# Edge sums of a graph network: packed bank offsets, edge weights moved to ScalarE, and 10 instead of 17 wide products of zeros in a pass

## The chip, the cores and the metric

One core of a Trainium2 chip runs the whole program. The metric is the device time of one launch in microseconds. TensorE multiplies, VectorE, ScalarE and GpSimd work on tiles in SBUF and PSUM, SyncE issues most DMAs. Each engine has a sequencer that reads its instructions in order.

## The reference

200,000 edges (src, dst) over 12,500 nodes with 64 features, three layers:

```python
f1 = relu(x[row] @ nb_W[l] + nb_b[l]); f2 = relu(x[col] @ self_W[l] + self_b[l])
h = relu(concat([f1, f2], 1) @ att1_W[l] + att1_b[l])
log_alpha = (h @ att2_W[l] + att2_b[l])[:, 0]
mask = clip(sigmoid(log_alpha) * (ZETA - GAMMA) + GAMMA, 0, 1)
rowsum = segment_sum(mask, row) + 1e-06
d = clip(rowsum ** -0.5, 0, 10)
vals = mask * d[row] * d[col]
x = segment_sum(vals[:, None] * x[col], row)
out = out + x
```

`row` is src, `col` is dst. The result is a layer norm of x + out.

## The kernel before

First the edges are sorted on the chip by their row, in blocks of 128 nodes, and padded, so that each tile of 128 edges has the rows of one block. This gives 1664 tiles. Eight tiles (U) make a step, four steps a pass of 32 tiles: QUADS is 52 passes per layer. `block_of` holds the block of each tile.

Each layer has three stages. The node stage makes per-node terms. The edge stage gathers them for each edge, makes the mask and, by one-hot products, the row sums. Between 9512 and 10576 us of the third layer, and at the same place of the others, stands the third stage, the edge sums. It is the stage that the change touches, and its loop is the pass of 32 tiles, called a lap here. A lap has three K steps (i = 0, 1, 2), whose edge rows x[col] were kept in DRAM (`kept_x`) and are loaded to `k_x`, and one G step, whose rows are gathered by GpSimd from `y_table` (already multiplied by d of the column). For a K step the engines do this:

- SyncE loads `k_cols` of step k+2, the column numbers of its edges (line 379), as soon as the look-up of step k-1 is done, and then `k_x` of step k (line 393).
- ScalarE (lines 683 and 687, steps i = 0 and 2) or VectorE (line 947, step i = 1) makes from them the transposed column one-hots `look_t` of step k+2.
- TensorE, `pick_rows` (line 564): 24 products of the one-hots with `d3`, which is d in three bf16 parts, in two halves. Each half goes to its own bank.
- VectorE, `look_up` (line 958): picks from each tile's bank the value of its column's high part and sums it, which is d of the column, into `k_weight`.
- VectorE, `weigh`: copies eight row numbers (967), multiplies `k_weight` by the mask (969) and makes for each tile a row one-hot times the weight (973), `k_hot`.
- TensorE, `sum_edges` (called at 601): for each of the eight tiles the product of `k_hot` and `k_x`, 128x64 in f32 (two passes each), added into a bank at a column offset. The offset is 64 times the tile's block less the first block of the step. The eight offsets stand in registers that `spots` fills from `spot_of` by one load of 16 (line 578) at i = 0 and one at i = 2.
- VectorE, `join` (981): adds the bank to `acc` at the step's first block, whose number comes by a register load of one.

The G step is like it, but ScalarE scales the gathered rows by the mask (672), in two halves, and VectorE makes one wide one-hot without weights (782). Its sum is the fourth of the lap (613).

Every bank is cleared by a product of zeros of 512 columns before its sum (`clear`). `stay_busy` adds such products into an unused bank. With four clears, and 2 + 2 in each K step and 1 before the G sum, a lap has 17 of them.

The order is the program order of each engine. In TensorE's lap: for each i: clears, sum of step k, register load at i = 0 and 2, pick of step k+2, at i = 1 the G sum, two products of zeros. VectorE's body for i: at i = 1 the G one-hot and the compare of line 947; look-up of step k+1; weigh of step k+1; join of step k-1; register load; at i = 2 the G join. ScalarE's and SyncE's bodies, and VectorE's, hold two laps (`B_BODIES`).

Of the kernel before, what the change touches and what calls it, by code (L numbers as in the profile page):

```python
# [26 lines left out]
I32 = mybir.dt.int32  # L27
ALU = mybir.AluOpType
# [27 lines left out]
def build(nc, x, src, dst, nb_W, nb_b, self_W, self_b, att1_W, att1_b, att2_W, att2_b, out):  # L56
# [53 lines left out]
    with ctx:  # L110
# [54 lines left out]
        spot_of = sb("spot_of", [1, TILES + 2 * U], mybir.dt.int16)  # L165
# [54 lines left out]
        def in_p3(shape, dt):  # L220
# [56 lines left out]
        k_rows, k_sel, k_wt, k_w, g_xs, k_acc = (  # L277
            sem("k_rows"), sem("k_sel"), sem("k_wt"), sem("k_w"), sem("g_xs"),
# [174 lines left out]
        def _(pe):  # L453
# [34 lines left out]
            spot = [[pe.alloc_register(f"pe_spot{h}_{k}") for k in range(2 * U)] for h in range(2)]  # L488

            with pe.Fori(0, LAYERS) as l:  # L490
# [85 lines left out]
                def spots(h, at):  # L576

                    pe.load(spot[h], spot_of[0:1, ds(at, 2 * U)])

                def sum_edges(to, j, hot, rows):  # L580
                    at = [pe.snap(r, min_val=0, max_val=(U - 1) * HID)
                          for r in spot[j // 2][j % 2 * U:(j % 2 + 1) * U]]
                    for k in range(U):
                        last = plus(to[:, ds(at[k], HID)], hot[:, k, :], rows[:, k, 0:HID])
                    return last
# [5 lines left out]
                spots(0, 0)  # L591
                with pe.Fori(0, QUADS) as b:
                    m = l * QUADS + b
                    for i in range(3):
# [3 lines left out]
                        stay_busy(2)  # L598
                        pe.wait_ge(k_w, l * (K_STEPS + 1) + k + 1)
                        pe.wait_ge(k_xin[i], (l * QUADS + (b + 1)) * 16)  # L600
                        sum_edges(bank[i], i, k_hot[i], k_x[i]).then_inc(k_o[i], 1)
                        if i == 0:
                            spots(1, (b * 4 + 2) * U)
                        if i == 2:
                            spots(0, (b * 4 + 4) * U)
                        pick_rows(b, i + 2)
                        if i == 1:
                            pe.wait_ge(g_acc, m)
                            clear(bank[3])
                            stay_busy(1)  # L610
                            pe.wait_ge(g_w, m + 1)
                            pe.wait_ge(g_xs, (m + 1) * 2)
                            sum_edges(bank[3], 3, g_hot, g_x).then_inc(g_o, 1)
# [5 lines left out]
        def _(act):  # L619
# [6 lines left out]
            with act.Fori(0, LAYERS) as l:  # L626
# [63 lines left out]
                with act.Fori(0, B_BODIES) as b:  # L690
                    for i in range(6):
                        if i % 3 != 1:
                            look_onehot(b, i + 2)

                        if i % 3 != 1:
                            continue
# [16 lines left out]
        def _(dve):  # L713
# [142 lines left out]
            v.memset(spot_of[0:1, TILES:TILES + 2 * U], 0)  # L856
            v.tensor_scalar(spot_of[0:1, 0:TILES], spot_of[0:1, 0:TILES], float(HID), None, ALU.mult).then_inc(s_edges, 1)
# [4 lines left out]
            with dve.Fori(0, LAYERS) as l:  # L862
# [101 lines left out]
                def weigh(i, k, at):  # L964

                    j = i % 2
                    v.tensor_copy(rows_now[j][:, :], row_lo[:, ds(at, U)]).then_inc(k_wt, 1)
# [99 lines left out]
```

## Time and profile before

| | |
|---|---|
| median of 3 runs | 10635.88 us (10630.31 to 10636.82) |
| the profiled execution | 10636.9 us |
| its span, first to last instruction | 10635.1 us |
| granted TensorE clock over the span | 0.62 |
| TensorE busy (products) | 6472.0 us, 61% |
| VectorE busy | 7981.6 us, 75% |
| ScalarE busy | 2043.5 us, 19% |
| GpSimd busy | 6098.0 us, 57% |

The times of all rows below are from the profiled execution. In them PE is TensorE, PEld its weight loads, DVE VectorE, ACT ScalarE, POOL GpSimd, SP SyncE; a q behind a name is that engine's sequencer or queue. A matmul's end is modelled in the profile, so the pace of TensorE is better read from the starts of its weight loads. A line's idle time stands in brackets before what ended it.

### The profile page before, as it was taken

To read this page: it belongs to the slowest core of one execution; us is meant where nothing else is said; L and a number is where in the kernel's file an instruction comes from. 1 tells how busy PE (TensorE), PEld (TensorE's weight loads), DVE (VectorE), ACT (ScalarE), POOL (GpSimd) and SP (SyncE) were. 2 spreads that over 40 slices of the span, in tenths; PEclk is the share of its full clock that TensorE was granted. 3 is DMA by queue.
4 is the path that set the end of the run, shared out by engine and by line. 5 is a ranking of instruction groups with operands and counts; after the bars stand their busy time and mean duration, and the time that the engine had idled before them with its cause. 6 is when DMAs were issued, how large, how long until landed. Compare 5 with 4: busy or idle time off the path is not lost.

```text
span 10635.1 us, 199487 instructions
## 1 busy us (share of the span) xinstructions
PE 6472.0 (61%) x45495; PEld 5622.2 (53%) x45814; DVE 7981.6 (75%) x33420; ACT 2043.5 (19%) x4175; POOL 6098.0 (57%) x6324
## 2 busy tenths in 40 slices
PE   3155555555588875555555568886555555558886
PEld 1145455555466665554554456665555555546665
DVE  8867777777688876777777678886777777768888
ACT  0021111111133331111111123333111111113332
POOL 0037777777533426777777733333777777753332
PEclk6565555555588885555555578887555555558887
DMA  0022223222533332222232443333222222253333
GB/s 20 0 55 72 72 71 71 72 71 71 80 90 90 90 83 68 71 72 71 72 71 70 67 94 90 92 88 71 72 72 71 72 71 72 71 81 90 90 90 75
DMA packets 921875, 778.06 MB, mean 73 GB/s; under 512 B 697300, under 2 KB 700660, under 8 KB 921460
## 3 DMA queue, kind: packets, MB, share of 16 engines
q0 software_dynamic: 199680, 368.45, 16.9%
q1 hardware_dynamic: 722164, 409.31, 14.1%
q14 instruction: 26, 0.21, 0.0%
q8 instruction: 5, 0.08, 0.0%
HBM read 620.19 MB, written 157.08 MB: 73 GB/s over the span
## 4 chain that ended last, share of the span: by engine, by line
PE 35%; POOL 23%; issue 21%; DVE 12%; DMA 6%; ACT 1%; ACTq 0%; DVEq 0%; POOLq 0%; SPq 0%
PE bank L459 12%; POOL k_hot L433 10%; POOL got L433 9%; PE bank L564 7%; PE bank L569 7%; PE bank L532 5%; DMA got<-qx_table,index 4%; POOL g_hot L433 4%; DVE acc L794 2%; DVE acc L795 2%; PE bank L522 1%; DVE hidden L906 1%; DVE hidden L904 1%; DVE small L909 1%; DMA k_hot<-qx_table,index 1%
## 5 line engine op out<-in xcount | busy, mean ns | idle before, releaser
L532 PE MATMUL bank<-p_all,onehot_t 128*128 x10032 | 2301.0, 424 | 1628.4 <-issue 1618.9
L532 PEld LDWEIGHTS bank<-p_all,onehot_t 128*128 128x128 f32 x10032 | 2186.3, 330 | 1679.4 <-issue 1679.4
L433 POOL DMA_INDIRECT got<-qx_table,index x2496 | 2395.1, 960 | 798.7 <-issue 762.4
L446 POOL DMA_INDIRECT got<-y_table,index x1248 | 1250.0, 1002 | 1967.8 <-ACT index L702 1456.9
L459 PE MATMUL bank<-mask,onehots 128*128 128x3 bf16 x4992 | 677.2, 184 | 1273.9 <-DVE mask L922 1273.8
L433 POOL DMA_INDIRECT k_hot<-qx_table,index x1248 | 1201.3, 963 | 380.4 <-issue 366.4
L433 POOL DMA_INDIRECT g_hot<-qx_table,index x1248 | 1200.9, 962 | 380.4 <-issue 377.6
L459 PEld LDWEIGHTS bank<-mask,onehots 128*128 128x128 bf16 x4992 | 519.3, 104 | 1544.9 <-issue 1436.8
L958 DVE SCALAR_TENSOR_TENSOR p_all<-iota_b,col_hi,bank 128x104 f32<-128x104 bf16 x3768 | 953.9, 317 | 442.7 <-PE bank L564 438.6
L564 PE MATMUL bank<-d,onehot_t 128*128 128x104 bf16 x11376 | 797.4, 243 | 621.5 <-issue 552.0
L654 ACT ACTIVATE small<-small 128x8 f32<-128x8 f32 x624 | 130.2, 209 | 5123.7 <-DVE small L911 5123.7
L564 PEld LDWEIGHTS bank<-d,onehot_t 128*128 128x128 bf16 x11376 | 724.3, 118 | 663.8 <-issue 593.4
L887 DVE TENSOR_SCALAR onehots<-iota_b,rows_now 128x128 bf16<-128x128 bf16 x5040 | 917.4, 289 | 22.5
L887 DVE TENSOR_SCALAR onehots<-iota_b,rows_b 128x128 bf16<-128x128 bf16 x5016 | 904.6, 284 | 22.0
L569 PE MATMUL bank<-zeros_b 128*128 128x512 bf16 x2340 | 795.2, 472 | 49.8 <-issue 41.4
L683 ACT ACTIVATE p_all<-p_all,minus_part 128x1024 bf16<-128x1024 bf16 x315 | 361.7, 1148 | 2155.0 <-DMA p_all<-col_rows 2154.9
L646 ACT CAST onehot_t<-bank 128x1024 f32<-128x1024 bf16 x630 | 637.6, 1012 | 412.6 <-PE bank L522 409.6
L904 DVE TENSOR_TENSOR hidden<-bank,got 128x512 f32<-128x512 f32 x312 | 215.7, 691 | 654.0 <-DMA got<-qx_table,index 654.0
L522 PE MATMUL bank<-ident_b,onehots 128*128 128x128 bf16 x5040 | 666.8, 314 | 7.9 <-DVE onehots L887 7.8
L522 PEld LDWEIGHTS bank<-ident_b,onehots 128*128 128x128 bf16 x5040 | 630.4, 164 | 8.9 <-DVE onehots L887 8.8
L421 POOL COPY x_step<-x_cur 128x256 f32 x78 | 50.3, 646 | 895.1 <-DVE b_cur L867 738.4
L569 PEld LDWEIGHTS bank<-zeros_b 128*128 128x128 bf16 x2655 | 295.7, 124 | 287.9 <-issue 209.8
(158 smaller groups left out, 9641.4 us busy)
## 6 DMA issues: line engine op xcount, KB each, us to landing
p_all<-col_rows SPq DMA_DIRECT2D x474, 256.0 KB, 3.5
kept_x<-got SPq DMA_DIRECT2D x312, 256.0 KB
k_x<-kept_x SPq DMA_DIRECT2D x312, 256.0 KB, 3.5
got<-qx_table,index POOLq DMA_INDIRECT x2496
kept_x<-g_hot SPq DMA_DIRECT2D x156, 256.0 KB
p_all<-kept_x SPq DMA_DIRECT2D x156, 256.0 KB
g_hot<-qx_table,index POOLq DMA_INDIRECT x1248
k_hot<-qx_table,index POOLq DMA_INDIRECT x1248
```

The source lines that it names most:

```text
L433: pool.indirect_dma_start(got[j][:, k, :], None, qx_table, bass.IndirectOffsetOnAxis(ap=index[j][:, k:k + 1], axis=0)).then_inc(a_got[j], 16)
L446: pool.indirect_dma_start(got[j][:, k, 0:HID], None, y_table, bass.IndirectOffsetOnAxis(ap=index[j][:, k:k + 1], axis=0)).then_inc(g_got[j ...
L459: return mm(to, lhsT, rhs, start=False, stop=True, skip_group_check=True)
L522: last = turn(bank_t[:, k, :], hot_a[j][:, k, :], ident_b[:, :])
L532: last = mm(bank_p[h][:, k, :], onehot_t[h][:, k, :], p_all[:, ds(ids[k], 1), :].rearrange("p o d -> p (o d)"), start=True, stop=True)
L564: last = mm(bank_d[n % 3][:, e, 0:NB], look_t[i % 3][:, q * (U // 2) + e, :], d3[:, s, :], start=(s == 0), stop=(s == 2))
L569: return mm(to[:, :], zeros_b[:, 0:PARTS], zeros_b[:, :], start=True, stop=True, skip_group_check=True)
L646: a.copy(onehot_t[h][:, :, :], bank_t).then_inc(a_trc, 1)
L683: a.activation(k_far, k_cols[c], ACT.Abs, bias=minus_part[:, :]).then_inc(k_away, 1)
L887: last = v.tensor_scalar(to[:, k, :], iota_b[:, :], rows[:, k:k + 1], None, ALU.is_equal)
L904: v.tensor_tensor(hidden[h][:, :, :], bank_p[h], got[j][:, :, 0:HID], ALU.add).then_inc(a_add[j], 1)
L958: last = v.scalar_tensor_tensor(out=picked[:, e, :], in0=iota_b[:, 0:NB], scalar=col_hi[:, ds(at + e, 1)], in1=bank_d[(2 * i + q) % 3][:, ...
```

## The change

Four edits, all in the third stage but for a few instructions of the setup:

1. The eight offsets of a step are packed into one 32-bit number, three bits each (`spots_of`, made by VectorE in the setup). `spots` loads four numbers, one for each step of the next lap, once a lap at i = 2. `sum_edges` shifts and masks the tile's offset out of the register before each product.
2. The weights leave the one-hots. VectorE makes one wide one-hot (`build_onehot`, as for the G step), joins, and only then multiplies `k_weight` by the mask (`weigh`). The copy of the row numbers is gone.
3. ScalarE scales the rows of `k_x` in place by those weights, in two halves, after its column one-hot. `sum_edges` waits for each half (`k_xs`), for the G step too (`g_xs`), where it waited for both at once.
4. Seven `stay_busy` products go: the two before each K sum and the one before the G sum.

```diff
-        spot_of = sb("spot_of", [1, TILES + 2 * U], mybir.dt.int16)
+        spot_of = sb("spot_of", [1, TILES], I32)
+        spots_of = sb("spots_of", [1, GROUPS + 4], I32)
...
-            spot = [[pe.alloc_register(f"pe_spot{h}_{k}") for k in range(2 * U)] for h in range(2)]
+            spot = [pe.alloc_register(f"pe_spot{j}") for j in range(4)]
...
-                def spots(h, at):
-
-                    pe.load(spot[h], spot_of[0:1, ds(at, 2 * U)])
-
-                def sum_edges(to, j, hot, rows):
-                    at = [pe.snap(r, min_val=0, max_val=(U - 1) * HID)
-                          for r in spot[j // 2][j % 2 * U:(j % 2 + 1) * U]]
+                def spots(b):
+                    pe.load(spot, spots_of[0:1, ds(b * 4, 4)])
+
+                def sum_edges(to, j, hot, rows, ready, half):
+                    of = pe.snap(spot[j], min_val=0, max_val=(1 << 3 * U) - 1)
+                    to_left = HID.bit_length() - 1
                     for k in range(U):
-                        last = plus(to[:, ds(at[k], HID)], hot[:, k, :], rows[:, k, 0:HID])
+                        bits = of >> (3 * k - to_left) if 3 * k > to_left else of << (to_left - 3 * k) if 3 * k < to_left else of
+                        at = pe.snap(bits & ((U - 1) * HID), min_val=0, max_val=(U - 1) * HID)
+                        if k % (U // 2) == 0:
+                            pe.wait_ge(ready, half + (k // (U // 2) + 1))
+                        last = plus(to[:, ds(at, HID)], hot[:, k, :], rows[:, k, 0:HID])
                     return last
...
                         clear(bank[i])
-                        stay_busy(2)
                         pe.wait_ge(k_w, l * (K_STEPS + 1) + k + 1)
-                        pe.wait_ge(k_xin[i], (l * QUADS + (b + 1)) * 16)
-                        sum_edges(bank[i], i, k_hot[i], k_x[i]).then_inc(k_o[i], 1)
-                        if i == 0:
-                            spots(1, (b * 4 + 2) * U)
+                        sum_edges(bank[i], i, k_hot[i], k_x[i], k_xs, (l * K_STEPS + k) * 2).then_inc(k_o[i], 1)
                         if i == 2:
-                            spots(0, (b * 4 + 4) * U)
+                            spots(b + 1)
                         pick_rows(b, i + 2)
                         if i == 1:
                             pe.wait_ge(g_acc, m)
                             clear(bank[3])
-                            stay_busy(1)
                             pe.wait_ge(g_w, m + 1)
-                            pe.wait_ge(g_xs, (m + 1) * 2)
-                            sum_edges(bank[3], 3, g_hot, g_x).then_inc(g_o, 1)
+                            sum_edges(bank[3], 3, g_hot, g_x, g_xs, m * 2).then_inc(g_o, 1)
...
+                        act.wait_ge(k_xin[i % 3], (l * QUADS + (b * 2 + (i // 3 + 1))) * 16)
+                        act.wait_ge(k_wt, l * (K_STEPS + 1) + b * 6 + (i + 1))
+                        scale_rows(k_x[i % 3], k_x[i % 3], lambda k: k_weight[i % 2][:, 1, k:k + 1], k_xs)
                         if i % 3 != 1:
                             continue
...
-            v.memset(spot_of[0:1, TILES:TILES + 2 * U], 0)
-            v.tensor_scalar(spot_of[0:1, 0:TILES], spot_of[0:1, 0:TILES], float(HID), None, ALU.mult).then_inc(s_edges, 1)
+            v.memset(spots_of[0:1, GROUPS:GROUPS + 4], 0)
+            packed = spots_of[0:1, 0:GROUPS].unsqueeze(2)
+            link(v.tensor_copy(packed, spots[:, :, U - 1:U]))
+            for k in reversed(range(U - 1)):
+                last = v.scalar_tensor_tensor(out=packed, in0=packed, scalar=8.0, in1=spots[:, :, k:k + 1],
+                                              op0=ALU.mult, op1=ALU.add)
...
-                def weigh(i, k, at):
-
-                    j = i % 2
-                    v.tensor_copy(rows_now[j][:, :], row_lo[:, ds(at, U)]).then_inc(k_wt, 1)
+                def weigh(j, k, at):
                     dve.wait_ge(k_sel, l * (2 * (K_STEPS + 1)) + k * 2 + 2)
                     v.tensor_tensor(k_weight[j][:, 1, :], k_weight[j][:, 0, :], mask[:, ds(at, U)],
                                     ALU.mult).then_inc(k_wt, 1)
-                    dve.wait_ge(k_wt, l * (2 * (K_STEPS + 1)) + k * 2 + 2)
-                    for e in range(U):
-                        last = v.tensor_scalar(k_hot[i % 3][:, e, :], iota_b[:, :], rows_now[j][:, e:e + 1],
-                                               k_weight[j][:, 1, e:e + 1], ALU.is_equal, ALU.mult)
-                    last.then_inc(k_w, 1)
...
                         look_up(i + 1, k + 1, next_at)
-                        weigh(i + 1, k + 1, next_at)
+                        build_onehot(k_hot[(i + 1) % 3], row_lo[:, ds(next_at, U)]).then_inc(k_w, 1)
                         join_last(b, i)
+                        weigh((i + 1) % 2, k + 1, next_at)
                         dve.load(k_blk, block_of[0:1, ds(at, 1)])
```

Two places in the order of instructions. The first is TensorE after the sum of step 0 in the loop over laps; ISA and REGISTER_ALU are work of the sequencer on registers. Before:

```order
L459 ISA
L459 MATMUL bank<-k_x,k_hot 128x64
L578 ISA
L578 TENSOR_LOAD spot_of
L556 ISA
L561 ISA
L564 MATMUL bank<-d,onehot_t 128x104 x12
L561 REGISTER_ALU
L564 MATMUL bank<-d,onehot_t 128x104 x12
L569 MATMUL bank<-zeros_b 128x512 x5
```

With the change:

```order
L461 REGISTER_ALU x2
L461 ISA
L461 MATMUL bank<-k_x,k_hot 128x64
L558 ISA
L563 ISA
L566 MATMUL bank<-d,onehot_t 128x104 x12
L563 REGISTER_ALU
L566 MATMUL bank<-d,onehot_t 128x104 x12
L571 MATMUL bank<-zeros_b 128x512 x3
```

The register load between sum and pick is gone here, two register operations stand before the tile's product, and of five products of zeros three are left.

The second place is VectorE from the last product of a look-up to the join, step 1 of the lap. Before:

```order
L967 ISA
L967 COPY rows_now<-row_lo 128x8
L968 REGISTER_ALU
L969 REGISTER_ALU
L969 TENSOR_TENSOR k_weight<-k_weight,mask 128x8
L973 TENSOR_SCALAR onehots<-iota_b,rows_now,k_weight 128x128 x8
L988 REGISTER_ALU
L979 ISA
L981 TENSOR_TENSOR acc<-acc,bank 128x512
```

With the change:

```order
L784 ISA
L784 TENSOR_TENSOR onehots<-iota_b,row_lo 128x1024
L989 REGISTER_ALU
L980 ISA
L982 TENSOR_TENSOR acc<-acc,bank 128x512
L974 REGISTER_ALU
L975 REGISTER_ALU
L975 TENSOR_TENSOR k_weight<-k_weight,mask 128x8
```

Eight instructions became one wide one, the copy went, and the multiply that makes the weights moved behind the join.

## Rows read from the trace of the kernel before

**Rows 1.** joins of VectorE in layer 3 (line 981): count, durations in ns, first and last start
```profile
L981 DVE TENSOR_TENSOR acc<-acc,bank x209: 667/679/690, 9511.9 to 10574.8; 128x512 f32 x105
```

**Rows 2.** busy time of each engine in the third stage of layer 3
```profile
9512.00:10576.00 1064.00, 866.17 (x7823) 732.45 (x7926) 893.85 (x4344) 339.99 (x673) 404.58 (x407) 0.86 0.34 88
```

**Rows 3.** timeline of TensorE's weight loads: start us, duration us, engine, line
```profile
3403.17 0.15 PEld L569 LDWEIGHTS bank<-zeros_b 128*128 128x128 bf16 x1 [0.28 <-issue]
...
3406.39 1.22 PEld L564 LDWEIGHTS bank<-d,onehot_t 128*128 128x128 bf16 x24
3407.55 0.14 PEld L569 LDWEIGHTS bank<-zeros_b 128*128 128x128 bf16 x2
3407.81 1.97 PEld L459 LDWEIGHTS bank<-onehots,g_hot 128*128 128x128 f32 x16
3409.65 0.86 PEld L569 LDWEIGHTS bank<-zeros_b 128*128 128x128 bf16 x5
3410.62 1.97 PEld L459 LDWEIGHTS bank<-p_all,onehots 128*128 128x128 f32 x16
3414.61 1.82 PEld L564 LDWEIGHTS bank<-d,onehot_t 128*128 128x128 bf16 x24 [2.02 <-issue]
...
3422.04 1.08 PEld L564 LDWEIGHTS bank<-d,onehot_t 128*128 128x128 bf16 x13 [1.83 <-issue]
```

**Rows 4.** register loads on the sequencers of TensorE (578, 527) and VectorE (1012)
```profile
L578 PEldq TENSOR_LOAD <-spot_of x315: 3782/3790/3853, 2858.0 to 10571.7; - x158
...
L527 PEldq TENSOR_LOAD <-block_of x627: 1917/1921/2282, 692.6 to 9465.2; - x157
...
L1012 DVEq TENSOR_LOAD <-block_of x468: 283/288/308, 2864.0 to 10571.4; - x156
```

**Rows 5.** who waited for whom, us in total, times, longest, 3200 to 3800
```profile
DVE p_all L958 <- PE bank L564: 78.9, 66, 2.7
```

**Rows 6.** register operations of TensorE's sequencer at line 459
```profile
L459 PEldq ALU_OP  x624: 32/34/42, 2862.7 to 10570.0; - x156
```

**Rows 7.** timeline of VectorE in one lap
```profile
3399.83 1.22 DVE L782 TENSOR_TENSOR g_hot<-iota_b,row_lo 128x1024 f32<-128x1024 bf16 x1
3400.97 0.48 DVE L947 TENSOR_SCALAR onehot_t<-p_all,part_f 128x1024 bf16<-128x1024 bf16 x1
3402.17 0.32 DVE L958 SCALAR_TENSOR_TENSOR p_all<-iota_b,col_hi,bank 128x104 f32<-128x104 bf16 x1 [0.73 <-PE bank L564]
...
3404.12 0.23 DVE L967 CAST rows_now<-row_lo 128x8 f32 x1
...
3404.53 2.13 DVE L973 TENSOR_SCALAR onehots<-iota_b,rows_now,k_weight 128x128 f32<-128x128 bf16 x8
3406.58 0.68 DVE L981 TENSOR_TENSOR acc<-acc,bank 128x512 f32 x1
```

**Rows 8.** timeline of ScalarE in one lap
```profile
3408.01 1.15 ACT L683 ACTIVATE p_all<-p_all,minus_part 128x1024 bf16<-128x1024 bf16 x1 [4.77 <-DMA p_all<-col_rows]
3409.26 1.15 ACT L687 ACTIVATE onehot_t<-p_all,one 128x1024 bf16<-128x1024 bf16 x1
3410.31 2.00 ACT L672 ACTIVATE onehots<-got,mask 128x64 f32<-128x64 f32 x8
3412.22 0.18 ACT L702 COPY index<-col_id 128x8 int32 x1
```

**Rows 9.** timeline of SyncE's DMA queue, one column load
```profile
3404.44 0.33 SPq L379 DMA_DIRECT2D p_all<-col_rows  x1
```

**Rows 10.** busy time and granted clock (before the last two) in single microseconds
```profile
3413.00:3414.00 1.00, 0.00 (x0) 0.00 (x0) 0.41 (x1) 0.00 (x0) 0.82 (x1) 1.00 0.07 27
...
3415.00:3416.00 1.00, 1.00 (x15) 1.00 (x13) 0.11 (x1) 0.00 (x0) 0.69 (x2) 0.50 0.02 4
```

**Rows 11.** timeline of TensorE's weight loads in the second stage
```profile
4110.29 3.49 PEld L532 LDWEIGHTS bank<-p_all,onehot_t 128*128 128x128 f32 x16 [2.97 <-issue]
```

**Rows 12.** the page's group of the gathers of y
```profile
L446 POOL DMA_INDIRECT got<-y_table,index x1248 | 1250.0, 1002 | 1967.8 <-ACT index L702 1456.9
```

More of the change, by code:

```diff
@@ L276, in build @@
         k_onehot = [sem("k_onehot_dve"), sem("k_onehot_act")]
-        k_rows, k_sel, k_wt, k_w, g_xs, k_acc = (
-            sem("k_rows"), sem("k_sel"), sem("k_wt"), sem("k_w"), sem("g_xs"),
+        k_rows, k_sel, k_wt, k_w, k_xs, g_xs, k_acc = (
+            sem("k_rows"), sem("k_sel"), sem("k_wt"), sem("k_w"), sem("k_xs"), sem("g_xs"),
             [sem(f"k_acc{c}") for c in range(3)])
@@ L590, in _ @@
                 clear(bank[2]).then_inc(k_o[2], 1)
-                spots(0, 0)
+                spots(0)
                 with pe.Fori(0, QUADS) as b:
@@ L855, in _ @@
             link(v.tensor_tensor(spots, by_step, by_step[:, :, 0:1].to_broadcast(steps_wide), ALU.subtract))
-            v.memset(spot_of[0:1, TILES:TILES + 2 * U], 0)
-            v.tensor_scalar(spot_of[0:1, 0:TILES], spot_of[0:1, 0:TILES], float(HID), None, ALU.mult).then_inc(s_edges, 1)
+            v.memset(spots_of[0:1, GROUPS:GROUPS + 4], 0)
[4 more added lines that the diff above has]
+                                              op0=ALU.mult, op1=ALU.add)
+                if k:
+                    link(last)
+            last.then_inc(s_edges, 1)
             dve.wait_ge(s_edges, 1)
@@ L992, in _ @@
                 look_up(0, 0, 0)
+                weigh(0, 0, 0)
                 for j in range(3):
                     dve.wait_ge(a_kept[j], (l + 1) * (16 * QUADS))
-                weigh(0, 0, 0)
+                build_onehot(k_hot[0], row_lo[:, 0:U]).then_inc(k_w, 1)
                 dve.wait_ge(l_end, l * 3 + 2)
```

## The prediction

> **What bounds the kernel now.** I read the page first, then the stages, then one lap of the last stage. VectorE is the busiest engine over the span, but the change touches only the third stage of each layer (the edge sums), so the shares over the span decide nothing. A lap is one pass of 32 tiles: three K steps (0, 1, 2) and one G step. The joins of layer 3 start from 9511.9 to 10574.8 us, 52 laps: 1062.9 / 52 = **20.44 us a lap**, and there are 156 laps [rows 1]. The window of that stage has a granted clock of 0.86, VectorE busy 894 of 1064 us, ScalarE 340 [rows 2]. No engine is full, so the limit is a chain or an engine with stalls that don't count as busy.
>
> TensorE is that engine. Start to start of its weight loads, at the full clock: a sum of eight tiles takes 1.84 us (3407.81 to 3409.65), a pick of 24 products 1.16 (3406.39 to 3407.55), a product of zeros 0.97 / 5 = 0.19. After the sum of step 2 it stands idle for 2.02 us and after that of step 0 for 1.83 us [rows 3]. Both follow a register load of 16 offsets: it holds the sequencer 3.79 us, a load of 8 takes 1.92, VectorE's load of one 0.29 [rows 4]. So a load costs 0.23 us a register; part is hidden because the sequencer had run ahead. The lap by these: 4 x 1.84 + 3 x 1.16 + 17 x 0.19 + 2.02 + 1.83 = 17.9. The clock gives the rest: 0.86 means that 0.28 of the lap, 5.7 us, runs at 1.2 GHz, which costs up to half of that, 2.9. Together at most 20.8, against 20.44 measured. VectorE waits for the picks, 78.9 us in 66 waits of a 600 us window [rows 5], which is the sign that TensorE leads.
>
> **The change, part by part.** All in the lap.
>
> 1. *Seven products of zeros fewer.* 7 x 0.19 = 1.3 us of TensorE at the full clock; at half clock one takes 0.43 (the row at 3403.17: 0.15 busy after 0.28 idle) [rows 3].
> 2. *One load of 4 registers for two of 16.* By 0.23 us a register the new load takes 0.98 us [rows 4]. That after step 0 is gone (1.83). After step 2 about 1.0 is left of 2.02: nothing is hidden any more, because the sequencer now waits for ScalarE in the middle of the sum. The values are now 4 bytes each. If bytes set the price, 16 bytes are as 8 of the old values, 1.92 us. I take the register count and keep 1.92 for a rival.
> 3. *Offsets unpacked on TensorE's sequencer.* Two register operations for each tile, 34 ns each [rows 6], so 0.07 us a tile against the 0.23 that a tile's passes take (1.84 / 8). The old sequencer ran a whole sum ahead, so its own pace is under that. From below they cost nothing, from above 8 x 0.07 = 0.5 us a sum, 2.2 a lap. I take nothing, except before the first tile.
> 4. *VectorE.* A step now is: look up 1.95 us (3402.17 to 3404.12), cast and multiply 0.41, eight weighted one-hots 2.05 (3404.53 to 3406.58), join 0.68. The cast goes, and the eight are one wide one-hot without weights, as the G step has: 1.14 (3399.83 to 3400.97) [rows 7]. New step: 1.95 + 1.14 + 0.68 + 0.17 = 3.94. The lap: 3 x 3.94, and in step 1 the G one-hot 1.14 and the wide compare 0.48, and a second join 0.68: 14.1 us. Its register load of 0.29 now stands behind the short multiply, with the join still running ahead of it, so it is covered.
> 5. *ScalarE.* Three times eight scalings of 128x64: 2.00 us each time, as its G scaling takes. With the G scaling 2.00, index copy 0.2 and two column one-hots of 1.25 + 1.15: 13.0 us a lap [rows 8]. It has room, but it is now in the chain: TensorE's sum waits for each half of the scaling (1.0 us), and the scaling waits for the weights, which VectorE now makes last, after its join. What queues behind the scaling on ScalarE is the next column one-hot. Its data come 3.57 us after the column load starts (3404.44 to 3408.01) [rows 8, 9], about two steps ahead of need, so it isn't late at 16 us a lap.
>
> TensorE's floor is then 7.36 + 3.48 + 10 x 0.19 + 1.0 = 13.7 us, VectorE's 14.1, ScalarE's 13.0. Three engines this close make the chain decide. From the moment when VectorE has the weights of step 1 (t = 0): ScalarE scales step 1 till 2.1, the G rows till 4.1, copies the index till 4.3, makes a column one-hot till 6.7, and has half of step 2 scaled at 7.7 and all at 8.7. TensorE was free at 6.9 (sum at 1.1 to 3.0, pick 4.2, G sum 6.2, zeros), so it waits 0.8. Its sum ends at 9.6; the sequencer issues the last tiles by 9.4 and loads till 10.4; the pick starts at 10.5, its first half is there at 11.1. VectorE, free at 10.2, starts the look-up at 11.2 and has the next weights 3.94 later: **15.1 us**. To that I add 0.4 for four hand-overs between engines, a tenth each by choice, and 0.5 for the clock.
>
> *The clock.* After the idle stretch that starts at 3412.6 the granted clock goes from 1.00 (window 3413) to 0.50 (window 3415) [rows 10], that is from 2.4 to 1.2 GHz, for about 3.4 us. The lap now has 1.7 such dips (5.7 / 3.4). After the change the idle stretches are 0.8, 1.0 and some 0.5 us. I take one dip a lap, 1.7 us of lost work, of which 0.5 reach the chain because TensorE waits anyway.
>
> The setup of the offsets is longer by some small operations on one partition, 2 to 4 us once; I put 2.
>
> The sum: 15.1 + 0.4 + 0.5 = 16.0 us a lap, 4.44 less than 20.44, times 156 = 693 us. The profiled execution took 10636.9 us (span 10635.1): 10636.9 - 693 + 2 = **9946 us**. The median of the runs is 1 us below the profiled one, which I leave out.
>
> The Trainium skill (TensorE: Matmul & The Clock Gate, What's actually happening) says that the default state is throttled and that activity releases it. This speaks against taking products out, and its result is the first rival. The same page (Architectural detail) gives TensorE a queue of 64 instructions; where the sequencer keeps that lead, as it did before, the new load would be hidden altogether and the lap would be 1.0 us shorter, 9790. The new waits inside each sum take the lead away, so I don't count on it; no row of before has such a wait.
>
> **The rivals.**
>
> - *The clock stays down (slower).* The zeros held the clock, and without seven of them it stays at 1.2 GHz. For it: one idle stretch of 2 us is enough to halve it now, and in the second stage, after an idle stretch of 2.97 us, sixteen weight loads take 3.49 us, where the sums now take half [rows 11]. Against: TensorE still works 13.7 of 16 us, a larger share than now (16.6 of 20.4). The price: a sum is then 3.49 us, a pick 1.82, a product of zeros 0.43 [rows 3]: 14.0 + 5.5 + 4.3 + 1.0 = 24.8 us, +4.36 x 156 = +680, so 11319 us. It decides from a mean clock below about 0.78: a 16 us lap reaches 20.44 with 8.9 us cold. Chance 0.07, with what lies between.
> - *Dips fall on the chain, one full dip a lap.* 15.5 + 1.7 = 17.2 us, 10133. For it: the two longest idle stretches are 2 us apart. Chance 0.18.
> - *The load is priced by bytes.* 1.92 for 0.98: 16.9 us, 10087. Chance 0.12.
> - *Unpacking is exposed.* The register operations delay each sum that starts late, up to 0.5 on three sums of the chain, and the byte price comes with it: 16.0 + 1.5 + 0.9 = 18.4 us, 10321. Chance 0.08.
> - *VectorE's floor.* The G scaling isn't ahead of step 2 in the steady order, and nothing but VectorE counts: 14.1 us, 9650. Against: its place in ScalarE's program is fixed. With half of it, 15.1 us or less, 9806. Chance 0.10.
> - *Nothing moves.* The gathers bound the stage. Eight a lap at 1.0 us [rows 12] are 8 us with gaps of 0.3 at most 10.4, so this could only be the wait for a slot. 10637. Chance 0.02.
>
> The forecast itself has 0.43. The range of 8 in 10 reaches from 9780 (14.9 us a lap) to 10290 (18.2); it leaves out most of the first and of the fifth rival, and the last. A measurement of this kernel can tell 0.2%, 21 us, from no change. Faster by more: 0.91. Within: 0.02. Slower: 0.07.
>
> **What would show it.** Joins 16 us a lap apart. No idle stretch after the sum of step 0, one of about 1.0 after that of step 2, and one load per lap of 0.98 us. A step of VectorE 3.9 to 4.0 us where it doesn't wait, with one wait a lap of about 1 us for the pick after step 2. ScalarE busy 13 of 16 us, its G scaling and column one-hot back to back before step 2. A clock of about 0.85 to 0.9 in the stage. The prediction is wrong if the clock there falls under 0.78, if the load takes 1.9 us, or if a sum takes over 2.2 us between its own waits.

## The result and the profile after

| | before | after |
|---|---|---|
| median of 4 runs each, side by side | 10635.5 us | 9854.9 us (9852.5 to 9856.5) |
| ratio, 95% interval | | 0.927 [0.925, 0.928] |
| span of the profiled execution | 10635.1 | 9850.6 |
| lap in layer 3 | 20.44 | 15.44 |
| granted clock in that stage | 0.86 | 1.00 |
| VectorE, ScalarE busy per lap there | 17.2, 6.5 | 13.5, 12.1 |

The change saves 780.6 us. The laps tell of all of it: (20.44 - 15.44) x 156 = 780. The forecast was 9946 us, 91 above the measured time, and the range 9780 to 10290 holds it.

The join's group of the changed kernel answers to [rows 1], and its window of the stage to [rows 2]: 9791.9 - 8989.0 = 802.9 us for 52 laps. The columns are range, us, PE, PEld, DVE, ACT and POOL busy, granted clock, DMA share, GB/s.

```profile
L982 DVE TENSOR_TENSOR acc<-acc,bank x209: 669/677/689, 8989.0 to 9791.9; 128x512 f32 x105
```

```profile
8989.00:9791.00 802.00, 773.03 (x7451) 675.47 (x7553) 703.16 (x3104) 631.61 (x1914) 443.84 (x409) 1.00 0.44 117
```

VectorE is now busy 703 of 802 us (88%), ScalarE 632 (79%), and the clock stands at its upper level, 2.4 GHz, throughout. The sequencer rows of TensorE answer to [rows 4] and [rows 6] (shortest/median/longest in ns):

```profile
L579 PEldq TENSOR_LOAD <-spots_of x159: 327/333/357, 2857.1 to 9791.5; - x159
...
L461 PEldq ALU_OP  x9360: 32/36/46, 2859.9 to 9791.1; - x200
```

Four numbers are loaded in 0.33 us, a third of what the forecast put. There are 9360 register operations where there were 624, 60 a lap, and each is on record with 36 ns (34 before). That number misleads, as the next view shows. The timeline of TensorE's weight loads in one lap, from sum 1 on, answers to [rows 3]:

```profile
9302.95 2.52 PEld L461 LDWEIGHTS bank<-k_x,p_all 128*128 128x128 f32 x16 [0.63 <-issue]
9305.42 1.13 PEld L566 LDWEIGHTS bank<-d,onehot_t 128*128 128x128 bf16 x24
9306.50 0.10 PEld L571 LDWEIGHTS bank<-zeros_b 128*128 128x128 bf16 x1
9306.55 2.19 PEld L461 LDWEIGHTS bank<-onehots,g_hot 128*128 128x128 f32 x16
9308.60 0.43 PEld L571 LDWEIGHTS bank<-zeros_b 128*128 128x128 bf16 x3
9309.19 2.52 PEld L461 LDWEIGHTS bank<-p_all,onehots 128*128 128x128 f32 x16 [0.16 <-issue]
9312.16 1.12 PEld L566 LDWEIGHTS bank<-d,onehot_t 128*128 128x128 bf16 x24 [0.45 <-issue]
```

A K sum takes 2.47 us from start to start (9302.95 to 9305.42), the G sum 2.05, where each took 1.84. The sequencer's own rows of the sum that starts at 9302.95 give count, durations in ns, first and last start:

```profile
L461 PEldq ALU_OP  x15: 32/36/36, 9302.7 to 9305.0; - x15
L461 PEldq FUSED_REGOPS  x8: 37/37/42, 9302.9 to 9305.1; - x8
```

These are 23 register operations in 2.4 us. They start 0.11 us apart, though each is on record with 0.04. A tile has up to three of them: the two new ones, and one (FUSED_REGOPS) that each tile had before. In the kernel before, that one is nearly all that a tile asks of the sequencer, and six of them in a row, for six tiles, start 0.1 us apart:

```profile
L459 PEldq FUSED_REGOPS  x6: 37/37/37, 3407.6 to 3408.1; - x6
```

So a tile takes the sequencer 0.31 us now (2.47 / 8), more than the 0.23 us of the tile's two passes, and TensorE waits for it inside the sum. The idle stretches of 2.02 and 1.83 us are gone: 0.45 us is left after the sum of step 2, where the load is, and 0.63 before sum 1.

VectorE's timeline answers to [rows 7]: the end of the weights of step 1, then the look-up after step 2's sum, and the next weights of step 1.

```profile
9301.37 0.16 DVE L975 TENSOR_TENSOR k_weight<-k_weight,mask 128x8 f32<-128x8 f32 x1
...
9313.15 0.32 DVE L967 SCALAR_TENSOR_TENSOR p_all<-iota_b,col_hi,bank 128x104 f32<-128x104 bf16 x1 [1.80 <-PE bank L566]
...
9315.11 1.22 DVE L784 TENSOR_TENSOR p_all<-iota_b,row_lo 128x1024 f32<-128x1024 bf16 x1
9316.25 0.67 DVE L982 TENSOR_TENSOR acc<-acc,bank 128x512 f32 x1
9316.84 0.15 DVE L975 TENSOR_TENSOR k_weight<-k_weight,mask 128x8 f32<-128x8 f32 x1
```

It waits once a lap, 1.80 us here, for the pick of step 4. ScalarE's part of that chain, which answers to [rows 8]:

```profile
9301.56 2.02 ACT L671 ACTIVATE k_x<-k_x,k_weight 128x64 f32<-128x64 f32 x8 [3.09 <-DVE k_weight L975]
9303.49 2.00 ACT L671 ACTIVATE onehots<-got,mask 128x64 f32<-128x64 f32 x8
9305.40 0.18 ACT L704 COPY index<-col_id 128x8 int32 x1
9305.48 1.15 ACT L682 ACTIVATE p_all<-p_all,minus_part 128x1024 bf16<-128x1024 bf16 x1
9306.73 1.15 ACT L686 ACTIVATE onehot_t<-p_all,one 128x1024 bf16<-128x1024 bf16 x1
9307.78 2.00 ACT L671 ACTIVATE p_all<-p_all,k_weight 128x64 f32<-128x64 f32 x8
```

From the weights at 9301.6 to the end of step 2's scaling at 9309.8 it works without a gap, in the order that the forecast walked.

### The profile page after: what moved, and what is told of

Same layout as the page of the kernel before. It is cut to its first block, busy times and chain, and to the rows that moved or that the text cites. A ratio compares the mean times of both kernels' runs of the same rounds, so it can differ in the third digit from the quotient of the medians.

```text
span 9850.6 us, 206958 instructions
## 1 busy us (share of the span) xinstructions
PE 6201.2 (63%) x44403; PEld 5462.9 (55%) x44722; DVE 7410.5 (75%) x29659; ACT 2922.9 (30%) x7919; POOL 6194.6 (63%) x6324
## 4 chain that ended last, share of the span: by engine, by line
PE 28%; POOL 25%; issue 19%; DVE 14%; ACT 8%; DMA 7%; ACTq 1%; DVEq 0%; POOLq 0%; SPq 0%
POOL k_hot L435 11%; PE bank L461 10%; POOL got L435 10%; PE bank L534 6%; PE bank L566 6%; DMA got<-qx_table,index 4%; POOL g_hot L435 4%; ACT p_all L671 3%; DVE acc L796 2%; DVE acc L797 2%; PE bank L571 2%; ACT onehot_t L686 2%; ACT p_all L682 2%; DMA k_hot<-qx_table,index 1%; PE bank L524 1%
## 5 line engine op out<-in xcount | busy, mean ns | idle before, releaser
L448 POOL DMA_INDIRECT got<-y_table,index x1248 | 1354.3, 1085 | 1163.7 <-ACT index L704 653.7
L671 ACT ACTIVATE k_x<-k_x,k_weight 128x64 f32<-128x64 f32 x2496 | 627.7, 334 | 476.9 <-DVE k_weight L975 476.9
L645 ACT CAST onehot_t<-bank 128x1024 f32<-128x1024 bf16 x630 | 637.6, 1012 | 418.1 <-PE bank L524 413.9
L566 PE MATMUL bank<-d,onehot_t 128*128 128x104 bf16 x11376 | 609.1, 211 | 117.3 <-DVE onehot_t L956 66.7
L566 PEld LDWEIGHTS bank<-d,onehot_t 128*128 128x128 bf16 x11376 | 541.7, 99 | 141.9 <-issue 70.3
L915 DVE SCALAR_TENSOR_TENSOR hidden<-hidden,a_cur 128x512 f32<-128x512 f32 x624 | 431.6, 692 | 21.2
L918 DVE TENSOR_REDUCE small<-hidden 128x8 f32<-128x512 f32 x624 | 428.0, 686 | 21.2
```

The costliest lines, as they stand in the source:

```text
L448: pool.indirect_dma_start(got[j][:, k, 0:HID], None, y_table, bass.IndirectOffsetOnAxis(ap=index[j][:, k:k + 1], axis=0)).then_inc(g_got[j ...
L566: last = mm(bank_d[n % 3][:, e, 0:NB], look_t[i % 3][:, q * (U // 2) + e, :], d3[:, s, :], start=(s == 0), stop=(s == 2))
L645: a.copy(onehot_t[h][:, :, :], bank_t).then_inc(a_trc, 1)
L671: last = a.activation(to[:, k, 0:HID], rows[:, k, 0:HID], ACT.Copy, scale=by(k))
L915: link(v.scalar_tensor_tensor(out=hidden[h][:, :, :], in0=hidden[h][:, :, :], scalar=0.0, in1=a2_cur[:, :].unsqueeze(1).to_broadcast([PART ...
L918: link(v.tensor_reduce(sm[:, 0, :], hidden[h][:, :, :], AX.X, ALU.add), e)
```

## The experiments

Each is the whole program, launched two to eight times beside the kernel before; the median is given. Laps are taken as above: first to last join of layer 3, by 52. The first three take the change apart.

### Zeros alone

To the kernel before:

```diff
                         clear(bank[i])
-                        stay_busy(2)
...
-                            stay_busy(1)
```

> The kernel before with 10 instead of 17 products of zeros a lap, nothing else. Theory A (TensorE leads before, and what halves its clock are the idle stretches after the two register loads of 16): the clock of the stage stays at 0.84 to 0.88, the lap falls by 1.3 to 2 us to about 18.8, 10380 us. Theory B (the zeros hold the clock up): the clock of the stage falls under 0.8 and the lap stays at 20.4 or grows, 10640 us or more.

Measured: 10633.1 us, ratio 1.000 [0.999, 1.001], lap 20.38.

```profile
9513.00:10572.00 1059.00, 834.42 (x7557) 751.25 (x7557) 894.32 (x4343) 341.87 (x674) 410.56 (x407) 0.80 0.34 89
```

The clock went from 0.86 to 0.80. At 0.80 the share of the lap at 1.2 GHz is 0.40, 8.2 us, where it was 5.7. The seven products save 7 x 0.19 = 1.3 us, and 2.5 us more at half clock cost up to half of that, 1.2. The idle time ahead of the picks grew too. In 400 us of this stage it was (us in total, times, longest), before and with the zeros gone:

```profile
PEld bank L564 <- issue: 76.0, 40, 2.1
```

```profile
PEld bank L564 <- issue: 93.0, 40, 3.4
```

That is 17 us in some 20 laps, 0.9 us a lap: a stretch after the load of step 0 is now up to 3.4 us long. That fewer products ahead of the load hide less of it would explain this, and was not tested. So the saving of 1.3 us went back as idle time and as clock, to within 0.1 us a lap; what share each has isn't separated. Theory A's saving did not come; the time and the direction of the clock are theory B's, but not that the clock alone explains it.

### Packed offsets alone

To the kernel before, with its 17 products of zeros and VectorE's weights:

```diff
-                    pe.load(spot[h], spot_of[0:1, ds(at, 2 * U)])
+                    pe.load(spot, spots_of[0:1, ds(b * 4, 4)])
...
+                        at = pe.snap(bits & ((U - 1) * HID), min_val=0, max_val=(U - 1) * HID)
```

> The kernel before with packed offsets alone (one load of 4 registers a lap, two register operations a tile), 17 products of zeros, weights in the one-hots. Theory A: without the two idle stretches of 2 us the clock of the stage is 1.00, TensorE no longer leads, and VectorE's floor of 3 x 5.09 + 1.62 + 0.68 = 17.6 us sets the lap at 17.7 to 18.2, about 10260 us. Theory B (the clock comes from the new order of waits or from ScalarE's part): the clock stays under 0.9 and the lap is 19 or more, 10420 us.

Measured: 10415.7 us, ratio 0.979 [0.977, 0.982], lap 19.01, load 0.332 us.

```profile
9369.00:10357.00 988.00, 887.32 (x7913) 741.77 (x7911) 883.99 (x4343) 340.58 (x674) 415.10 (x407) 0.90 0.37 96
```

```profile
9705.54 2.56 PEld L460 LDWEIGHTS bank<-k_x,k_hot 128*128 128x128 f32 x16 [0.45 <-issue]
...
9714.71 3.49 PEld L460 LDWEIGHTS bank<-k_x,p_all 128*128 128x128 f32 x16 [2.36 <-issue]
```

Time and lap are as theory B gave them (19 or more, 10420 us), with a clock of 0.90, at the edge of what it said. It laid the clock of 1.00 to the new order of waits or to ScalarE's part; of the rise from 0.86, 0.04 come without them, and the next run shows that they alone don't bring it either. The load is cheap, but the loads of weights of a K sum at full clock take 2.56 us here too, with no wait inside it. So the unpacking, and not the wait for ScalarE's halves, makes the sums longer. After the longest idle stretch of this view, 2.36 us, a sum takes 3.49, the same as [rows 11]. VectorE has 884 us of 988 to do, 17.0 a lap, so there is little to gain under that.

### ScalarE's weights alone

To the changed kernel, and with 17 products of zeros:

```diff
-        spot_of = sb("spot_of", [1, TILES], I32)
-        spots_of = sb("spots_of", [1, GROUPS + 4], I32)
+        spot_of = sb("spot_of", [1, TILES + 2 * U], mybir.dt.int16)
...
+                    pe.load(spot[h], spot_of[0:1, ds(at, 2 * U)])
...
+                        if i == 0:
+                            spots(1, (b * 4 + 2) * U)
                         if i == 2:
-                            spots(b + 1)
+                            spots(0, (b * 4 + 4) * U)
```

> The kernel before with the weights on ScalarE alone: wide one-hots, multiply behind the join, half waits in the sums; loads of 16 registers and 17 products of zeros as before. Theory A: the sequencer now stops in each sum, so each load of 3.79 us lies open after its sum, the idle stretches grow from 2 to 3.5 us and the lap to 22 or 23, about 10950 us, slower than before. Theory B (the weights on VectorE were the bound, TensorE's stalls were slack): the lap falls to 18 or less, 10260 us.

Measured: 10630.0 us, ratio 1.000 [0.999, 1.001], lap 20.23.

```profile
9501.00:10553.00 1052.00, 866.56 (x7925) 724.16 (x7926) 713.88 (x3104) 645.77 (x1916) 414.31 (x410) 0.87 0.34 90
```

```profile
9809.33 1.12 PEld L565 LDWEIGHTS bank<-d,onehot_t 128*128 128x128 bf16 x24 [2.10 <-issue]
...
9821.36 0.78 PEld L565 LDWEIGHTS bank<-d,onehot_t 128*128 128x128 bf16 x14 [2.01 <-issue]
```

VectorE lost 180 us of work in this stage (894 to 714) and the time stands still. The idle time behind the load is 2.10 us after step 0 (1.83 before) and 2.01 after step 2 (2.02 before): the load holds TensorE as before, at nearly the same clock. Theory B's 18 us did not come, nor did theory A's 22: in laps as long as these the new waits inside the sums don't take away what the sequencer had run ahead. The loads of 3.79 us were what bounded the lap, and VectorE was the next limit, 17.2 us. Lifting the second alone gives nothing.

### Is it the number of registers, or the kind of number?

The load of four 32-bit numbers took 0.33 us, where 0.23 us a register would give 0.9. This kernel is the one before with another type and nothing else.

```diff
-        spot_of = sb("spot_of", [1, TILES + 2 * U], mybir.dt.int16)
+        spot_of = sb("spot_of", [1, TILES + 2 * U], I32)
```

> The kernel before with the offsets held as 32-bit instead of 16-bit numbers, still two loads of 16 registers a lap. Theory P (a load costs 0.23 us a register whatever its type, and only the count fell with the packing): the load takes 3.8 us, the time is 10636. Theory Q (the width of the number decides, as 4 of 32 bits took 0.33 us and 1 of 16 bits 0.29): the load takes 1.4 us or less, the idle stretches after it close, the clock of the stage goes to 1.00 and the lap to VectorE's 17.6 to 18.2, about 10260 us, with no packing.

Measured: 10173.8 us, ratio 0.957 [0.954, 0.960], lap 17.45.

```profile
L578 PEldq TENSOR_LOAD <-spot_of x315: 1102/1106/1127, 2856.8 to 10109.8; - x158
```

```profile
9207.00:10115.00 908.00, 791.95 (x7923) 647.45 (x7920) 884.84 (x4345) 340.54 (x674) 421.63 (x408) 0.97 0.39 104
```

Sixteen numbers of 32 bits load in 1.11 us, sixteen of 16 bits in 3.79. One word in the program gives more than twice what packing gives alone, 2.99 us a lap against 1.43. Theory Q, by which the kind of number sets the price, is right, though the clock is 0.97 and not 1.00. VectorE is then full: 885 of 908 us.

### Unpacking ahead of the sum

To the changed kernel: the shifts and masks of all eight tiles stand before the sum's first wait for ScalarE, but after the wait for VectorE's one-hots, and go into registers of their own.

```diff
+                    for k in range(U):
+                        by = 3 * k - to_left
+                        if by:
+                            pe.reg_alu(offset[k], spot[j], abs(by),
+                                       ALU.logical_shift_right if by > 0 else ALU.logical_shift_left)
+                        pe.reg_alu(offset[k], offset[k] if by else spot[j], (U - 1) * HID, ALU.bitwise_and)
+                    at = [pe.snap(r, min_val=0, max_val=(U - 1) * HID) for r in offset]
...
-                        last = plus(to[:, ds(at, HID)], hot[:, k, :], rows[:, k, 0:HID])
+                        last = plus(to[:, ds(at[k], HID)], hot[:, k, :], rows[:, k, 0:HID])
```

> The changed kernel with all eight offsets of a step unpacked into registers before the first wait for ScalarE. Theory U (in the changed kernel a K sum takes 2.5 us instead of 1.84 because the register operations stand between the products): the sum falls to 1.85 to 2.0 us between the starts of its weight loads, the lap from 15.44 by 0.5 to 1.0 us, about 9740 us. Theory H (the wait for the second half of the scaling stretches the sum): the sum stays at 2.4 or more and the time at 9855.

Measured: 10090.4 us, ratio 0.949 [0.946, 0.952], lap 16.94: slower than after by 235 us.

```profile
9505.08 1.96 PEld L461 LDWEIGHTS bank<-k_x,k_hot 128*128 128x128 f32 x16 [1.65 <-issue]
...
9514.36 1.86 PEld L461 LDWEIGHTS bank<-onehots,g_hot 128*128 128x128 f32 x16 [1.18 <-issue]
9517.57 1.86 PEld L461 LDWEIGHTS bank<-p_all,onehots 128*128 128x128 f32 x16 [1.05 <-issue]
```

The sums are back at 1.86 us, so the register operations did stretch them, as theory U has it; its time, 9740 us, did not come. Now 1.05 to 1.65 us of idle stands ahead of these sums, more than was taken out (the sum of step 1 has 0.28 in this lap and 1.10 in others). The masks (line 589) ahead of the sum at 9505.08, and the one operation that follows them:

```profile
L589 PEldq ALU_OP  x8: 32/36/36, 9503.2 to 9504.5; - x8
```

```profile
L590 PEldq FUSED_REGOPS  x1: 182/182/182, 9504.6 to 9504.6; - x1
```

From the start of the first mask to that of the last are thirteen steps, seven masks and six shifts, in 1.3 us: 0.10 us an operation, where 0.036 is on record. All fifteen take 1.4 us and the one behind them 0.18, before the first product can go. In this order that is the sequencer's time whether it stands inside the sum or ahead of it. Unpacking ahead of the wait for VectorE's one-hots was not run.

### More and fewer zeros in the changed kernel

The changed kernel with 17:

```diff
                         clear(bank[i])
+                        stay_busy(2)
...
+                            stay_busy(1)
```

> The changed kernel with 17 products of zeros again. Theory A (the clock is held by the missing idle stretches): the clock of the stage stays 1.00; the two products before a K sum partly fill a wait of 0.2 to 0.6 us, so the lap grows by 0.2 to 0.6 us, 9890 to 9950 us. Theory C (taking the zeros out is where the gain came from): the lap grows by 1.3 us or more, 10060 us.

And with 4, the clears alone:

```diff
-                        stay_busy(2)
```

> The changed kernel with the four clears alone, no other product of zeros. Theory A: idle stretches stay under 1.3 us, the clock stays at 0.95 or more, and the lap falls by 0 to 0.3 us, 9810 to 9855 us. Theory B (the zeros hold the clock): the clock of the stage falls under 0.85 and the lap grows by 1 us or more, over 10010 us.

Measured: 9857.3 us with 17 (ratio 0.927 [0.925, 0.930], lap 15.48) and 9890.3 us with 4 (0.930 [0.928, 0.933], lap 15.67). The window with 17 zeros, then that with 4:

```profile
8991.00:9796.00 805.00, 783.07 (x7821) 682.08 (x7923) 703.67 (x3104) 631.66 (x1914) 445.92 (x410) 1.00 0.43 117
```

```profile
9014.00:9829.00 815.00, 756.97 (x7196) 682.34 (x7247) 704.98 (x3105) 631.60 (x1914) 439.53 (x410) 0.93 0.43 116
```

```profile
9411.42 2.52 PEld L461 LDWEIGHTS bank<-k_x,p_all 128*128 128x128 f32 x16 [0.96 <-issue]
```

Theory A is right that the clock stays at 1.00 with 17, but the lap grows by 0.04 us and not by 0.2 or more. With 4 neither came: theory A had a clock of 0.95 or more and a gain, theory B one under 0.85. Between 17 and 10 there is nothing to gain or lose: TensorE has time for them in its waits, and the clock is 1.00 either way. Below 10 the idle time ahead of a sum grows (0.96 us where 10 zeros left 0.63), the clock falls to 0.93, and the lap is 0.23 us longer, 36 us in 156 laps.

### No packing: eight 32-bit numbers ahead of each sum

To the changed kernel; the offsets stay in `spot_of`, as 32-bit numbers, and the step's tile number is the argument:

```diff
-                def sum_edges(to, j, hot, rows, ready, half):
-                    of = pe.snap(spot[j], min_val=0, max_val=(1 << 3 * U) - 1)
+                def sum_edges(to, tile, hot, rows, ready, half):
+                    pe.load(spot, spot_of[0:1, ds(tile, U)])
+                    at = [pe.snap(r, min_val=0, max_val=(U - 1) * HID) for r in spot]
...
-                            spots(b + 1)
```

> The changed kernel without packing: eight 32-bit offsets are loaded before each sum's wait for ScalarE, no unpacking. Theory Q (four 32-bit numbers come in one access of about 0.3 us): the load of 8 takes 0.6 us or less and lies in the wait, a sum takes 1.85 to 2.0 us, no load stands between sum and pick; the lap falls by 0.6 to 1.3 us to 14.2 to 14.8, about 9700 us. Theory P (0.23 us a register): the load takes 1.9 us four times a lap, the lap is 18 us or more, 10260 us.

Measured: 9653.5 us, ratio 0.908 [0.905, 0.911], lap 14.15.

```profile
L578 PEldq TENSOR_LOAD <-spot_of x624: 587/592/637, 2858.1 to 9589.1; - x156
```

```profile
8857.00:9593.00 736.00, 689.34 (x7474) 594.76 (x7578) 703.59 (x3105) 631.66 (x1914) 465.96 (x410) 1.00 0.48 128
```

```profile
9300.90 1.92 PEld L460 LDWEIGHTS bank<-k_x,p_all 128*128 128x128 f32 x16 [0.44 <-issue]
```

Four loads a lap of 0.59 us are 2.4 us of the sequencer's time, in part under the work of the step ahead, and the weight loads of a K sum are at 1.92 us. In 400 us the idle time ahead of the sums is

```profile
PEld bank L460 <- issue: 67.4, 113, 1.0
```

which is 2.4 us a lap in four stretches of up to 1.0, and the clock is 1.00 all the same. The lap is 1.29 us shorter than the change's, and again on theory Q's side. VectorE is now busy 704 of 736 us (96%).

### ScalarE's weights with wide numbers, loaded in two sixteens

To the kernel with ScalarE's weights alone:

```diff
-        spot_of = sb("spot_of", [1, TILES + 2 * U], mybir.dt.int16)
+        spot_of = sb("spot_of", [1, TILES + 2 * U], I32)
```

> ScalarE's weights with 17 products of zeros and two loads of 16 offsets a lap, as in the run with ScalarE's weights alone, but the offsets are 32-bit, so a load takes 1.1 us. Theory V (once the loads are cheap, VectorE's 17.1 us of work a lap is what is left to take away): the lap falls from 20.2 to 14.8 to 15.6 us, about 9800 us, and the clock is 1.00. Theory W (ScalarE's part costs TensorE its lead, so a load after a sum still lies open): the lap stays over 16.5 us, 10020 us or more.

Measured: 9799.0 us, ratio 0.922 [0.920, 0.924], lap 15.10.

```profile
8951.00:9736.00 785.00, 737.90 (x7925) 639.43 (x7925) 704.90 (x3104) 631.82 (x1915) 454.79 (x410) 1.00 0.44 120
```

Against the kernel of 17 zeros with packed offsets (15.48) only the way to the offsets differs: packing is 0.38 us a lap dearer than two loads of sixteen. The lap and the clock of 1.00 are theory V's. With the weights off VectorE, the one-word edit takes the lap from 20.23 to 15.10. The laps of the profiled executions side by side, all with 17 products of zeros:

| offsets | VectorE's weights | ScalarE's weights |
|---|---|---|
| 16 bits, two loads | 20.44 | 20.23 |
| packed | 19.01 | 15.48 |
| 32 bits, two loads | 17.45 | 15.10 |

Packing gives 1.43 us by itself, the weights 0.21, both 4.96. The 0.21 is not clear of noise: by the medians (10635.5 and 10630.0) the weights alone give 0.04 us a lap. Two thirds of the gain belong to neither alone.

### The column one-hots of another step

VectorE is full at 14.15, and its wide compare stood in step 1, beside the G one-hot. This kernel moves it: VectorE makes it in step 2 and ScalarE in steps 0 and 1. To the kernel of eight 32-bit numbers, in ScalarE's body and then in VectorE's:

```diff
-                        if i % 3 != 1:
+                        if i % 3 != 2:
                             look_onehot(b, i + 2)
...
+                        if i % 3 == 2:
+                            look_onehot(b, i + 2)
```

> The run with eight 32-bit offsets loaded before each sum, and in it the column one-hots rotated: VectorE makes that of step 1 modulo 3 instead of step 0, ScalarE those of steps 0 and 2, so that ScalarE makes one in the 1.8 us in which it waits for the weights of step 1 and has none between its G scaling and step 2. Theory K (the chain through ScalarE to the pick after step 2 holds VectorE 0.5 us a lap): the lap falls from 14.15 to 13.6 to 13.8 us, 9570 to 9600 us. Theory L (VectorE's own issue sets the lap): it stays at 14.1, 9650 us.

Measured: 9622.4 us (9618.5 to 9623.6), ratio 0.905 [0.903, 0.907], lap 13.91.

```profile
8838.00:9562.00 724.00, 691.39 (x7571) 589.76 (x7571) 706.74 (x3104) 643.50 (x1914) 453.96 (x408) 1.00 0.48 130
```

This lies between what theories K and L gave, and is the fastest kernel here, 0.976 of the change. VectorE is busy 707 of 724 us, 98%, and that is what bounds it: its own work is 13.6 us a lap, and only less of it would help further. The waits of VectorE for the pick in 400 us (us in total, times, longest), without and with the rotation:

```profile
DVE p_all L950 <- PE bank L565: 14.0, 28, 0.5
```

```profile
DVE p_all L950 <- PE bank L565: 3.8, 18, 0.2
```

## Why the prediction was right, and where it was not

**The mechanism held.** TensorE led with stalls that don't count as busy, the loads made them, and after the change a chain over three engines sets the lap. The walk against the trace, in us from the end of the weights of step 1 (9301.53):

| event | forecast | measured |
|---|---|---|
| sum 1 starts | 1.1 | 1.4 |
| ready for sum 2 (G sum and zeros done) | 6.9 | 7.5 |
| sum 2 starts | 7.7 | 7.7 |
| pick of step 4 starts | 10.5 | 10.6 |
| look-up starts | 11.2 | 11.6 |
| next weights of step 1 done | 15.1 | 15.5 |

The forecast had 15.1 and 0.4 for hand-overs, 15.5, and the lap is 15.44. Two of its terms were wrong inside that and cancelled, which is luck, and one did not.

**The clock term failed.** "I take one dip a lap, 1.7 us of lost work, of which 0.5 reach the chain." There is none: the granted clock of the stage is 1.00. Without that term the lap is 15.5 and the time 9946 - 0.5 x 156 = 9868, 13 us from the measured. The idle stretches that remain, 0.45 and 0.63 us, cost no clock. With 4 zeros they grow to 0.96 and 0.31 ahead of the sums and the clock is 0.93. The sign given for the stage, a clock of 0.85 to 0.9, was wrong for the same reason.

**The load was mis-sized.** "By 0.23 us a register the new load takes 0.98 us": it takes 0.33. Rows of 16-bit numbers alone [rows 4] set that price, and the step took a change of type as harmless. The rival that priced by bytes is out in the other direction: wider numbers load faster, 1.11 us for sixteen against 3.79. The idle stretch after the sum of step 2 is 0.45 us and not 1.0. "Nothing is hidden any more, because the sequencer now waits for ScalarE in the middle of the sum" is not settled as the cause. With those waits and no unpacking, the load of 3.79 us leaves 2.01, as before, and that of 1.11 leaves 0.8 (first row: ScalarE's weights with wide numbers). With the unpacking and without the waits, the load of 0.33 leaves the same 0.45 in some laps (second row: packed offsets alone). So either can take the sequencer's lead, and the changed kernel has both.

```profile
9600.65 1.12 PEld L565 LDWEIGHTS bank<-d,onehot_t 128*128 128x128 bf16 x24 [0.84 <-issue]
```

```profile
9703.23 1.12 PEld L565 LDWEIGHTS bank<-d,onehot_t 128*128 128x128 bf16 x24 [0.45 <-issue]
```

**Unpacking was not free.** "I take nothing, except before the first tile", from 0.07 us a tile against 0.23. A K sum became 2.47 us, 0.63 more; the bound from above, 0.5, was too low as well. "The prediction is wrong if a sum takes over 2.2 us between its own waits" has come true for this step. What failed is the reading of a duration on record as the time that an operation takes of its sequencer: the starts stand 0.10 us apart, not 0.034. The two new operations add 0.2 us a tile to the 0.1 that the sequencer took before, which is over the 0.23 of the passes. The rival that had unpacking exposed was right in this and priced it at 0.5 us a sum, but the byte price that it came with did not come. On sum 2, which is on the chain, the load's 0.65 us less and the sum's 0.63 us more cancel. Sum 1, the G sum and their zeros come 0.6 later, which fell into the 0.8 us that TensorE would have waited there: 0.16 of it is left.

**VectorE and ScalarE were right.** A step of VectorE from the look-up that waited to the next weights is 3.84 us (forecast 3.94), ScalarE is busy 12.1 us of the lap (forecast 13.0), with its G scaling and column one-hot back to back before step 2. The one wait of VectorE a lap is there, but 1.8 us long where about 1 was forecast.

**The seven zeros.** The part "7 x 0.19 = 1.3 us of TensorE" holds for TensorE's time, and none of it is in the result: 9857 us with 17, 9855 with 10. It has to be read with the other parts, since in the kernel before it was given back, as idle time after a load and by the clock. The Trainium skill (TensorE: Matmul & The Clock Gate, What's actually happening) says that activity releases the clock. Its direction is seen twice, with seven zeros fewer in the kernel before (0.86 to 0.80) and six fewer in the changed one (1.00 to 0.93). The rival built on it, a stage that stays at 1.2 GHz for want of seven products, is out.

**Two parts that need each other.** The prediction priced the parts in one walk and did not ask what each gives alone. The table shows it: two limits stood at nearly the same height, TensorE's loads (17.9 us and the clock) and VectorE's work (17.2). Each part lifts one.

**Left open.** How an idle stretch and the products around it share in the clock is not settled. The length of a stretch alone does not set it: stretches of up to 1.0 us went with a clock of 1.00 in the kernel of eight 32-bit numbers, which has 10 zeros, and one of 0.96 with 0.93 in the kernel of 4. That a register operation takes 0.10 us is read from the starts; what the sequencer does in the 0.06 that no duration covers, no row shows. The dearer 16-bit load is measured, its cause is not.

## What to carry to other kernels

Look at the type of what a sequencer loads before packing it or loading less of it: here one word, 16 bits to 32, gave more than the packing did, and made the rest of the change work. Charge register operations at what a stretch of them takes from start to start, not at the duration on record. Where two limits stand close together, expect nothing of a part alone, and judge zeros that hold a clock again after the idle stretches they were put there for are gone.

## What the runs showed of the hardware

- Register loads on TensorE's sequencer: 3.79 us for sixteen 16-bit numbers, 1.92 for eight; of 32-bit numbers 1.11 for sixteen, 0.59 for eight, 0.33 for four. That is 0.23 a number of 16 bits, and of 32 bits some 0.065, with about 0.07 once.
- Register operations of TensorE's sequencer are on record with 36 ns and start 0.10 to 0.11 us apart, in the sums of the changed kernel and in the run that has them ahead of the sum.
- The granted clock of a stage with stretches of 0.45 to 0.63 us of idle a lap was 1.00, with stretches of 2 us 0.86, and with one of 2.36 us (packed offsets alone) the sum behind it took 3.49 us, where another took 2.56. With stretches of up to 1.0 us it was 1.00 in the kernel of eight 32-bit numbers.
- Products of zeros moved the clock only where it had already fallen or the idle stretches grew with their going: 0.86 to 0.80 from 17 to 10 in the kernel before, 1.00 to 1.00 for the same step in the changed one, 0.93 with 4.
